# Attention and feed-forward on one core: scores in four PSUM banks instead of three, maxima in three instead of four, and a new order on TensorE

## The reference

```
logits  = q k^T / 4                       # per batch and head, 2048 x 2048
attend  = |i - j| <= 128  or  i == 0  or  j == 0
weights = softmax(where(attend, logits, -inf))
out     = (weights v) Wo^T
```

## Time and profile before

| | |
|---|---|
| median of 3 runs | 1142.13 us (1135.82 to 1143.86) |
| the profiled execution | 1144.1 us, its span 1142.3 us |
| granted TensorE clock, mean | 0.985 of 2.4 GHz |
| PE, DVE, ACT, POOL busy | 97%, 82%, 68%, 61% of the span |

### The profile page before, as it was taken

One profiled execution on the slowest core, in us unless ns is written; L12 is line 12 of the kernel. 1 busy time (PEld: TensorE's weight loads), 2 busy tenths in 40 slices (PEclk: granted clock), 3 DMA queues, 4 the chain that ended last, 5 costly groups with the idle time before them and its releaser, 6 DMA issues. The chain is left out here.

```text
span 1142.3 us, 31735 instructions
## 1 busy us (share of the span) xinstructions
PE 1109.0 (97%) x11867; PEld 732.5 (64%) x11867; DVE 939.7 (82%) x3233; ACT 772.1 (68%) x1321; POOL 692.2 (61%) x916
## 2 busy tenths in 40 slices
PE   9999998999999999999999999879999999999998
PEld 8888884344444444444444444348888988898887
DVE  7889855898888888888888988557888788888885
ACT  7989983577777777777777777745565456555654
POOL 3665558377777877887777877844344334433443
PEclk9999997799999999999999999989999999999999
DMA  6999998457554656565556654140331123111201
GB/s 197 293 297 280 270 245 208 94 123 161 119 139 112 136 140 155 129 139 121 127 131 158 133 137 102 35 135 1 94 91 56 57 67 100 56 56 57 74 20 38
DMA packets 189674, 145.15 MB, mean 127 GB/s; under 512 B 61240, under 2 KB 189264, under 8 KB 189520
## 3 DMA queue, kind: packets, MB, share of 16 engines
q1 hardware_dynamic: 189520, 143.12, 49.2%
HBM read 91.32 MB, written 50.95 MB: 125 GB/s over the span
## 5 line engine op out<-in xcount | busy, mean ns | idle before, releaser
L1590 ACT ACTIVATE a_weights<-e_psum 128x1024 f32<-128x1024 f32 (+1 forms) x512 | 395.1, 809 | 150.3 <-PE e_psum L1506 146.5
L1641 DVE CUSTOM_DVE_ANT_0 a_masked<-e_psum,band 128x290 f32<-128x290 f32 (+8 forms) x1024 | 405.0, 445 | 74.4 <-PE e_psum L1482 65.1
L1417 POOL TENSOR_SCALAR_AFFINE_SELECT a_weights<-a_weights 128x1024 f32<-128x1024 f32 x256 | 270.9, 1093 | 9.7 <-ACT a_weights L1590 9.7
L1866 POOL TENSOR_TENSOR f_square<-f_relu 128x512 f32<-128x512 f32 x128 | 147.3, 1152 | 208.4 <-ACT f_relu L1855 187.4
L1506 PE MATMUL e_psum<-e_q,e_k 128*128 128x384 bf16 (+2 forms) x1408 | 234.3, 283 | 4.9 <-ACT a_weights L1590 3.2
L1482 PE MATMUL e_psum<-e_k,e_q 96*32 96x290 bf16 (+2 forms) x4096 | 226.5, 293 | 3.6 <-PEq L285 2.8
L1528 PE MATMUL e_psum<-a_weights,a_v 128*17 128x384 f32 (+2 forms) x2816 | 220.3, 394 | 5.9 <-DVE e_turned L1280 5.1
L1506 PEld LDWEIGHTS e_psum<-e_q,e_k 128*128 128x128 bf16 x1408 | 96.8, 98 | 158.6 <-ACT a_weights L1590 75.9
L1482 PEld LDWEIGHTS e_psum<-e_k,e_q 96*32 96x32 bf16 x4096 | 86.2, 96 | 112.9 <-issue 52.9
L1822 PE MATMUL e_psum<-w_w_t,f_square_hi 128*128 128x256 f32 x512 | 129.3, 287 | 5.7 <-DVE f_square_lo L1912 5.7
L1824 PE MATMUL e_psum<-w_w_t,f_square_lo 128*128 128x256 f32 x512 | 126.7, 282 | 0.0
(11 more groups left out here) (218 smaller groups left out, 1894.3 us busy)
## 6 DMA issues: line engine op xcount, KB each, us to landing
k_parts<-p_k_parts SPq DMA_DIRECT2D x48, 258.0 KB, 4.7
e_k<-k_parts SPq DMA_DIRECT2D x64, 193.5 KB, 3.6
e_k<-k_parts SPq DMA_DIRECT2D x192, 64.5 KB, 3.3
q_parts<-p_q_parts SPq DMA_DIRECT2D x48, 256.0 KB, 5.5
e_q<-q_parts SPq DMA_DIRECT2D x64, 192.0 KB, 3.7
e_q<-q_parts SPq DMA_DIRECT2D x192, 64.0 KB, 3.2
v_ones<-p_va SPq DMA_DIRECT2D x16, 544.0 KB, 5.8
p_x<-in_x SPq DMA_DIRECT2D x16, 512.0 KB, 6.8
```

What stands on the lines that cost most here:

```text
L1417: pool.affine_select(out=blocks, in_=blocks, compare_op=ALU.is_ge, fill=0.0, base=0, pattern=[[0, NQ // 2 * HEAD_COLS // P // CUT_STEP], [ ...
L1590: act.activation(pe_w[:, us.upar, lo:hi], score[c % 2][:], ACT.Exp).then_inc(s_exp, 1)
L1641: dve.tensor_tensor_reduce(out=masked[:, place + lo:place + hi], in0=bank[:, lo:hi], in1=band[:, lo:hi], scale=1.0, scalar=NEG, op0=ALU.ad ...
L1866: pool.tensor_tensor(sh.r2[:, j % 4, :], sh.r[:, j % 4, :], sh.r[:, j % 4, :], ALU.mult).then_inc(self.s_sq, 1)
```

## The change

The score banks are grouped otherwise: the twelve banks of a unit are now six pieces of 1024 columns (two banks each, across the limits of the heads), which take turns in PSUM banks 0-1 and 2-3. For that the maxima give up bank 3 and turn through banks 5, 6 and 7, counted on from unit to unit. ScalarE does six exponents of 1024 columns where it did four of 1024 and four of 512. GpSimd's first cut waits for three pieces, where it waited for four of the smaller; that is the same half of the weights. TensorE's order is new: runs of two, four, two, two and two score banks, and sum 0 two tiles earlier.

```
-CHUNK_COLS = ((0, 2 * GT), (2 * GT, HEAD_COLS))
-CHUNKS = 2 * NQ
+CHUNK = 2 * GT
+CHUNKS = NQ * HEAD_COLS // CHUNK
...
-TURN_BANKS = 4
+TURN_BANKS = 3
...
-    (), (("score", 2),), (), (), (("score", 3), ("score", 4), ("score", 5)),
-    (), (), (("sum", 0),), (("score", 6), ("score", 7), ("sum", 1)),
...
+    (), (), (("score", 2), ("score", 3), ("score", 4), ("score", 5)), (), (),
+    (("sum", 0), ("score", 6), ("score", 7)), (), (), (("score", 8), ("score", 9), ("sum", 1)), (("sum", 2),), (),
...
-        self.score = [psum[:, 0:2, :].rearrange("p a n -> p (a n)"), psum[:, 2, :]]
-        self.sum_bank, self.turn = self.banks[4], [self.banks[i] for i in (3, 5, 6, 7)]
+        self.score = [psum[:, 2 * i:2 * i + 2, :].rearrange("p a n -> p (a n)") for i in range(2)]
+        self.sum_bank, self.turn = self.banks[4], self.banks[5:8]
...
-    def tile_bank(self, j):
-        return self.turn[j % TURN_BANKS]
+    def tile_bank(self, u, j):
+        return self.turn[(u.n * TILES + j) % TURN_BANKS]
...
-                    if third == 0:
-                        wait(pe, s_exp, us.n * CHUNKS + 2 * h - 1)
-                    if third == 2:
-                        wait(pe, s_exp, us.n * CHUNKS + 2 * h)
+                    piece, second = divmod(n, 2)
+                    if not second:
+                        wait(pe, s_exp, us.n * CHUNKS + piece - 1)
...
-                    if third >= 1:
+                    if second:
                         ins.then_inc(s_score, 1)
...
-                        lo, hi = (c // 2 * HEAD_COLS + x for x in CHUNK_COLS[c % 2])
-                        act.activation(pe_w[:, us.upar, lo:hi], score[c % 2][:], ACT.Exp).then_inc(s_exp, 1)
+                        act.activation(pe_w[:, us.upar, c * CHUNK:(c + 1) * CHUNK], score[c % 2][:], ACT.Exp).then_inc(s_exp, 1)
```

More of the change, by code:

```diff
@@ L879 @@
 AFTER_TILE = (
-    (), (("score", 2),), (), (), (("score", 3), ("score", 4), ("score", 5)),
-    (), (), (("sum", 0),), (("score", 6), ("score", 7), ("sum", 1)),
-    (), (("sum", 2),), (("score", 8), ("score", 9), ("score", 10)),
-    (), (), (("sum", 3), ("score", 11), ("sum", 4)), (("sum", 5),))
+    (), (), (("score", 2), ("score", 3), ("score", 4), ("score", 5)), (), (),
+    (("sum", 0), ("score", 6), ("score", 7)), (), (), (("score", 8), ("score", 9), ("sum", 1)), (("sum", 2),), (),
+    (("score", 10), ("score", 11), ("sum", 3)), (), (("sum", 4),), (("sum", 5),), ())
 def in_group(gi, kb):
@@ L1481, in max_tile @@
                     for h in range(NQ):
-                        ins = pe.matmul(sh.tile_bank(j)[h * SUB:(h + 1) * SUB, lo:hi],
+                        ins = pe.matmul(sh.tile_bank(ux, j)[h * SUB:(h + 1) * SUB, lo:hi],
                                         qw[ux.q][0:SLOT_ROWS, h, j * SUB:(j + 1) * SUB],
@@ L1504, in score_bank @@
                         k0 = (us.gi * TB + kb) * KPITCH + 1
-                        c0 = third % 2 * GT + col * P
+                        c0 = second * GT + col * P
                         ins = pe.matmul(
-                            score[third // 2][:, c0:c0 + m * P],
+                            score[piece % 2][:, c0:c0 + m * P],
                             kt[us.hq][:, h, k0:k0 + P],
                             qw[us.q][:, h, qb * P:(qb + m) * P], start=True, stop=True)
-                    if third >= 1:
+                    if second:
                         ins.then_inc(s_score, 1)
@@ L1633, in body @@
                         start, lo, hi = keys_of(ux.gi, j)
-                        bank, place = sh.tile_bank(j), masked_place(ux, j)
+                        bank, place = sh.tile_bank(ux, j), masked_place(ux, j)
                         if j == 0:
```

## The result

The changed kernel takes 1205.4 us (median of 4 runs, 1200.68 to 1209.05), the kernel before 1142.99 us on the same chips: a ratio of 1.055, 95% interval 1.049 to 1.062. The profiled execution has a span of 1198.8 us against 1142.3, so 56.5 us of difference to find; the changed kernel's is the shortest of its four.

The account below looks back on a forecast made before the run. Two nearly equal limits: TensorE's work and a loop from sum 0 through reciprocal, `o` and cuts. The loop's 1.14 us less 0.06 slack, times 59, adds 64 us: 1206 us, 8-in-10 range 1187 to 1221.

Parts of the forecast that it names:

- Two limits of nearly the same length: Attention stage before: TensorE's own work and a loop of waits through VectorE, GpSimd and TensorE; period 8.54 us.
- The loop after the change: From sum 0 through j10, j11, reciprocal, `o` and cuts to the next sum 0: 9.70 us, 1.14 more.
- the constant part: From the reciprocal's start through `o` and the cuts to the next sum 0: instructions unchanged, 5.25 us.
- The 0.11 us for a further tile: TensorE's start-to-start distance for each further tile in a group, read from the profile before.
- the estimate that the prediction set aside: Trainium skill's rule for matmuls on different column tiles: 0.13 us for a further tile, about 2 us in all.
- The mean: Mean growth of the attention period: 1.14 us less 0.06 of old slack, 1.08 us, 59 times.
- The ends of the stage: First and last iterations of the attention stage: costed at nothing, 3 us either way.
- Three banks at zero: Three banks for the maxima: no wait on the path behind sum 0, so zero; bound one VectorE tile, 0.38 us.
- Rival 1: TensorE alone sets the period: 1130 us, or 1147 with the exponent's wait uncovered; 8%.
- the exponent's wait: Third piece of scores waits 0.2 to 0.3 us for the first's exponent; free if covered, otherwise up to 18 us.
- Rivals 2 and 4: Three banks bind between sum 0 and j10: 1229 us, 6%; the loop grows less, by 0.8: 1189 us, 7%.
- Rival 3: TensorE's clock falls through idle of 1.1 us each period, one iteration in five at half clock: 1246 us, 5%.

Follow-up runs that it names:

- E4: Kernel before, with VectorE's reciprocal behind tile j13 instead of j11, nothing else: 1227.3 us, ratio 1.073 to the kernel before.
- E2: Kernel before, with VectorE's reciprocal behind tile j6 instead of j11, nothing else: 1136.4 us, ratio 0.995 to the kernel before.
- E3: Changed kernel, with VectorE's reciprocal behind tile j6 instead of j11, nothing else: 1133.3 us, ratio 0.993 to the kernel before.
- E9: E6 with VectorE's two-input operation of the shift behind tile j6 instead of j4: 1156.3 us, ratio 1.012 to the kernel before.
- E1: Changed kernel with TensorE's old order; new pieces and three banks for the maxima stay: 1164.2 us, ratio 1.020 to the kernel before.
- E5: Kernel before, with three banks for the maxima instead of four, nothing else: 1164.7 us, ratio 1.019 to the kernel before.
- E6: Changed kernel with sum 0 back behind tile j7 instead of j5, all else as changed: 1167.0 us, ratio 1.024 to the kernel before.
- E8: The E4 kernel run once more for its profile: 1224.9 us, a single execution.

## Why the prediction was right

- **The bound.** "Two limits of nearly the same length" held. E4 shows that the loop sets the time when it is lengthened, E2 that cutting it in the kernel before gives only 5 us, because TensorE's own work lies just below.
- **The loop after the change.** Step by step, predicted and measured: sum 0 to scores 0.77 and 0.77; two score banks 0.54 and 0.54; three tiles then scores 0.47 and 0.49; sum 1 0.23 and 0.23; j9 0.14 and 0.13; sum 2 0.65 and 0.65; j10 on VectorE after 0.35 and 0.35; j11 and the reciprocal 0.38 and 0.38 each; the constant part 5.25 and 5.25. In all 9.70 and 9.71 us. The 0.11 us for a further tile was low by the rounding of two rows: one, two and three tiles ahead of scores take 0.24, 0.36 and 0.49 us here (432.47, 430.09 and 428.05 in the changed kernel), so a further tile is 0.12 to 0.13, nearer the 0.13 of the estimate that the prediction set aside. It moves the loop by 0.02 us.
- **The mean.** 8.54 + 1.08 gives 9.62, measured 9.64. The slack of the old loop, 0.06, was thus about right.
- **The ends of the stage**, costed at nothing with 3 us either way, gave back 4.1 and 3.1 us in the two profiled executions. By the medians (62.4 us more, 63.7 of them by the periods) they gave back 1.3. The four executions of the changed kernel span 8 us, so that the median came within 1 us of the 1206 is in part luck. The start is not the change's: the first reciprocal stands between 228.0 us (E3) and 237.6 (E9) with the same work ahead of it, and it goes with the clock granted between 190 and 228 us, 0.86 in E3, 0.82 in the changed kernel, 0.70 in the kernel before and 0.62 in E9. The part behind the last reciprocal is 410.8 us in E1 and 414.0 in E5, which differ in the pieces alone; that the new pieces shorten it by 3 us is likely and, with one execution of each, not shown.
- **Three banks at zero** was right for this order and no other. The prediction looked at the tiles behind sum 0 and found room. It did not say that the price sits ahead of sum 0, where E1, E5 and E6 pay it: with sum 0 behind j5 no tile ahead of it needs a bank that is read after the cuts' end, and sum 0 follows the cuts by 0.05 or 0.06 us in every iteration read, with the two-input operation or without. The two changes to the order thus pull against each other, and the earlier sum 0 bought freedom from the bank with a longer loop.
- **Rival 1** (TensorE alone sets the period) is refused by E4 and by the wait in 48 of 48 iterations. Its number, 1130 without and 1147 with the exponent's wait uncovered, is where E3 arrives once the loop is gone: 1133.
- **Rivals 2 and 4** (the banks bind on the path, the loop grows by less) are refused by the same steps: none of them from sum 0 to j10 holds a wait of a tile's 0.38 us, and the period grew by 1.10 us and not by 0.8.
- **Rival 3** (the clock falls) happened once in the 58 periods of the profiled execution. The stretch 484 to 488 us:

```profile
484.00:488.00 4.00, 3.12 (x23) 0.73 (x23) 1.99 (x8) 1.54 (x3) 2.69 (x6) 0.61 0.07 10
```
```profile
484.88 1.49 PE L1526 MATMUL e_psum<-a_weights,a_v 128*17 128x384 f32 x8 [1.11 <-POOL a_weights L1416]
```

The granted clock is 0.61 there, mostly the 1.2 GHz level, after 1.11 us of idle, sum 0 takes 1.49 us instead of 0.84, and that period is 11.11 us instead of 9.60. It cost 1.5 us, where the rival priced twelve such periods at 40 us. The Trainium skill, "TensorE: Matmul & The Clock Gate", section "A second HAM failure mode: psum-queue depth-cycling", tells of a kernel whose clock swings between two levels because TensorE idles briefly between groups of matmuls. This trace doesn't bear that out for this kernel: every period has about 1 us of idle at sum 0, and the clock fell in one.

## What to carry to other kernels

When two waits in the list are each other's neighbours (A waits for B's result, and B's engine for one behind A), add the distances once round: if the sum equals the period, it is a loop, and its length, not any engine's load, is the time. Then the place of a small instruction that hands the loop on matters more than the layout of the big ones: look for one that stands behind work it doesn't need, here a reciprocal of 0.25 us that stands behind five tiles more than in E3. And judge a change of buffers and a change of order together, since the value of a buffer is that of the one place where the order needs it.

## What the runs showed of the hardware

- A VectorE operation with two inputs in SBUF that starts during one of GpSimd's cuts ends with that cut: by 0.04 to 0.05 us behind it in all 22 of E6 between 300 and 700 us. It lasts 0.21 us (median in E3, where the cuts are over by then) and 0.83 in E6. It waits for the one cut that is running and not for all four: in E6 and E1 it meets the last cut of the row, in E8 mostly the third, and ends while the fourth runs. VectorE and GpSimd in E8:

```profile
494.01 1.13 DVE L1629 SCALAR_TENSOR_TENSOR a_neg_rest<-a_max_turned,a_shift 128x32 f32<-128x32 f32 x1
```
```profile
491.92 4.22 POOL L1417 TENSOR_SCALAR_AFFINE_SELECT a_weights<-a_weights 128x1024 f32<-128x1024 f32 x4
```

  Each cut takes 1.09 us and they start 1.04 or 1.05 apart, so the third runs from 494.01 to 495.10 and the fourth from 495.05 to 496.14. The operation ends at 495.14, 0.04 behind the third. VectorE's tiles, with one input in PSUM, keep their 0.46 us beside the same cuts (421.30 in E6, cuts from 418.11 to 422.34), and the cuts keep their 4.23. The Trainium skill, "GPSIMD Engine Reference", section "Specifications", says that GpSimd shares its SBUF interfaces with VectorE, with contention for VectorE instructions with two SBUF inputs; the traces agree, and show it as waiting to the end of the running cut.
- TensorE's distances from start to start hold from kernel to kernel to 0.02 us. A sum is followed by scores about 0.11 us later than by a tile (0.55 against 0.44 us after a sum of 256 queries), and so is a tile (0.24 against 0.13). A run of one score bank takes 0.32 us to the next tile and a run of two 0.54 (543.97 to 544.29 and 543.07 to 543.61 in the kernel before), so a bank is 0.22 and the run has 0.10 more. A change between tiles and sums costs 0.02 or less: sums of 384, 256 and 128 queries take 0.65, 0.44 and 0.23 us to the next tile, 0.21 for each 128 queries.
